# Second layer's keys with values and both query kinds from products of 256 columns, recurrent queries with keys in one; part of VectorE's work on ScalarE

## Time and profile before

| | |
|---|---|
| median of 3 runs | 369.15 us (365.88 to 369.27) |
| profiled execution | 368.68 us, span of its instructions 367.0 us |
| mean granted TensorE clock | 0.863 |
| TensorE matmul, weight load | 299.7 us (82%), 210.4 us |
| VectorE | 243.5 us (66%) |
| ScalarE | 187.5 us (51%) |
| GpSimd | 147.0 us (40%) |

### The profile page before, as it was taken

How to read it: one execution, slowest core, us unless ns; L and a number is a source line. 1 busy time by engine, 2 the same in 40 slices (tenths; PEclk the granted TensorE clock), 3 DMA queues, 4 the chain that set the end, 5 groups by cost and what they waited for, 6 DMA issues and landing times.

```text
span 367.0 us, 7990 instructions
## 1 busy us (share of the span) xinstructions
PE 299.7 (82%) x2646; PEld 210.4 (57%) x2646; DVE 243.5 (66%) x697; ACT 187.5 (51%) x392; POOL 147.0 (40%) x225
## 2 busy tenths in 40 slices
PE   0556898288899987768989889987688999999993
PEld 0432444145559965555645455454445877999993
DVE  5779757288977777589867879999899013431124
ACT  1447987238656541232153676576116775646450
POOL 4955788951133452393024223244562110100272
PEclk9985999799979996678555998999657999999999
DMA  6997000000000660000000000000012625543122
GB/s 199 334 348 329 0 3 2 0 2 1 2 2 0 232 231 0 0 1 2 0 2 0 3 2 2 2 3 8 30 43 68 203 81 159 158 145 87 34 54 80
DMA packets 21383, 26.14 MB, mean 71 GB/s; under 512 B 1816, under 2 KB 16672, under 8 KB 20832
## 3 DMA queue, kind: packets, MB, share of 16 engines
q1 hardware_dynamic: 20576, 24.07, 20.6%
q0 software_dynamic: 768, 1.57, 1.5%
HBM read 19.15 MB, written 6.49 MB: 70 GB/s over the span
## 4 chain that ended last, share of the span: by engine, by line
PE 34%; DVE 12%; issue 6%; ACT 2%; POOL 2%; DMA 2%; SPq 1%; POOLq 1%; DVEq 0%; ACTq 0%
PE single L1668 4%; PE single L1324 4%; PE single L1331 4%; DVE mx L1117 3%; PE double L1371 2%; POOL tmp L787 2%; PE double L1679 2%; PE double L1531 2%; PE single L1679 2%; PE outs L1420 2%; PE double L1527 2%; PE double L1324 1%; PE double L1331 1%; PE double L1596 1%; PE outs L1428 1%
## 5 line engine op out<-in xcount | busy, mean ns | idle before, releaser
L865 ACT ACTIVATE region_p<-double 128x1024 f32<-128x1024 f32 x64 | 63.6, 1030 | 26.8 <-PE double L1371 11.8
L751 POOL TENSOR_SCALAR_AFFINE_SELECT region_p<-region_p 128x512 f32<-128x512 f32 (+1 forms) x48 | 38.8, 808 | 55.7 <-ACT region_p L865 54.3
L1117 DVE TENSOR_REDUCE mx<-double 128x4 f32<-128x1024 f32 (+1 forms) x24 | 29.4, 1226 | 4.5 <-PE double L1531 3.7
L709 POOL TENSOR_SCALAR rstd<-mv 128x2 f32<-128x2 f32 x24 | 5.8, 240 | 65.5 <-DVE mv L990 64.6
L997 DVE TENSOR_SCALAR xn<-x,mv,rstd 128x128 f32<-128x128 f32 x64 | 24.7, 499 | 6.3 <-POOL rstd L715 4.4
L787 POOL DMA_INDIRECT tmp<-moved,spots x12 | 11.5, 961 | 33.9 <-issue 33.5
L1104 DVE TENSOR_REDUCE mxc<-double 128x16 f32<-128x1024 f32 x16 | 19.6, 1225 | 7.8 <-PE double L1511 7.2
L1331 PE MATMUL single<-wb,xnT 128*128 128x128 f32 (+2 forms) x112 | 22.1, 325 | 3.2 <-ACT xnT L820 2.0
L744 POOL TENSOR_SCALAR kcm<-kcT,cst 128x1024 f16<-128x1024 f16 x8 | 22.9, 2863 | 0.8
L1420 PE MATMUL outs<-region_p,vst 128*32 128x256 f32 x256 | 22.9, 440 | 0.2 <-issue 0.2
L1331 PEld LDWEIGHTS single<-wb,xnT 128*128 128x128 f32 x112 | 17.6, 224 | 8.9 <-issue 7.5
(11 more groups left out here) (342 smaller groups left out, 771.5 us busy)
## 6 DMA issues: line engine op xcount, KB each, us to landing
tmp<-in_experts SPq DMA_DIRECT2D x11, 514.0 KB, 3.5
w<-in_experts SPq DMA_DIRECT2D x4, 1024.0 KB, 6.4
moved<-yb SPq DMA_DIRECT2D x1, 3840.0 KB, 17.6
w<-in_w1a SPq DMA_DIRECT2D x2, 1024.0 KB, 15.3
w<-in_w2a SPq DMA_DIRECT2D x2, 1024.0 KB, 10.3
xl<-moved SPq DMA_DIRECT2D x19, 64.0 KB, 3.1
moved<-yb SPq DMA_DIRECT2D x19, 64.0 KB, 2.2
wb<-in_wb SPq DMA_DIRECT2D x1, 837.0 KB, 8.5
```

The lines of the kernel that those rows point to most:

```text
L751: then(g.affine_select(out=v, in_=v, compare_op=ALU.is_ge, fill=0.0, base=0, pattern=[[0, n], [1, P]], channel_multiplier=-1), "prob_masked")
L865: a.activation(probs[:, slot("prob", key), :], psum(step), ACT.Exp, scale=SCALE).then_inc(psum_done[PSUM.slot(step)], 1)
L1117: gives(step, v.tensor_reduce(dst, psum(step).rearrange("p (r g k) -> p r g k", r=2, k=k), X, ALU.max))
```

## The change

- `k4` and `v4` become one step `k4` with a moving operand of 256 columns; VectorE makes the key stack, then ScalarE copies the values out with two instructions. `q4` and `qc4` become one step `q4`: one product of 256 columns, after which VectorE builds both stacks; `tq` of either kind waits for both stacks.
- The biases of the values of both cross attentions and of layer 1's self attention are no longer added to the values: two new steps `vb.1` and `vb.4` push them through the output weights and add them to the output bias, once. `kcv` is then two copies instead of eight additions.
- Norms 3, 4 and 6 (`SCALED`): the normed tiles are made by ScalarE as `x * rstd + offset`; GpSimd makes `offset = -mean * rstd` with two more instructions.
- `p3a` is one product with a 128x128 weight; ScalarE takes out both halves.
- The output gate is `0.5 * tanh(z / 2) + 0.5`: one ScalarE and one VectorE instruction. `mxe` has two instructions instead of three.
- `LENGTHS` has new numbers and more kinds, and `ORDER_OF_STEPS` is a new list. In it ropea.3 and ropea.1 (square roots) stand behind the first exponentials; kcx.1 stands between sc.0.0.5 and sc.0.2.0 (before: between sc.0.3.0 and sc.0.3.1); the mixture of layer 0 for sequences 1 and 3 (fup.2, fup.3, fdown.2, fdown.3) stands inside the recurrent block of 0 and 2 (before: ahead of it). The last steps are nearly the same.

```diff
+SCALED = (3, 4, 6)
-        parts = [("D", 0.9 if twice else 0.5)] + ([("G", 0.7)] if s in (1, 3, 4) else [])
+        parts = [("A" if s in SCALED else "D", 0.9 if twice else 0.5)] + ([("G", 0.7)] if s in (1, 3, 4) else [])
...
+                    if s in SCALED:
+                        mean = mv[:, h, tiles(b), 0].unsqueeze(1).to_broadcast([P, n, 2])
+                        o = offset[:, h, 0:n, tiles(b)]
+                        then(g.tensor_tensor(o, mean, r[:, 0:n], ALU.mult))
+                        then(g.tensor_scalar(o, o, -1.0, None, ALU.mult), "rstd_ready")
...
+                if kind == "lnb" and step[1] in SCALED:
+                    act.wait_ge(sem("rstd_ready"), count(("lna",), ("lna", s, b)))
+                    for n, dst in enumerate((h, 1 - h) if s in AGAIN else (h,)):
+                        for t in tiles_of(b):
+                            ins = a.activation(xn[:, dst, t, :], x[:, t, :], ACT.Identity,
+                                               bias=offset[:, h, n, t:t + 1], scale=rstd[:, h, n, t:t + 1])
...
+                elif kind == "k4":
+                    after_scalar(act, step)
+                    act.wait_ge(sem("presets4"), 4 * count(("presets4",), ("presets4", b)))
+                    for q in range(2):
+                        a.activation(v4[:, tiles(b), q, :, 16 * q:16 * q + HD],
+                                     two(psum(step))[:, :, P:T].rearrange(
+                                         "p i (q h e) -> p i q h e", q=2, e=HD)[:, :, q], ACT.Copy).then_inc(
...
+                    evac(step, kT3[:, slot("mlstm", b), :], psum(step)[DH:2 * DH, 0:T])
...
-                    then(a.activation(og3[:, w], og3[:, w], ACT.Exp, scale=-1.0), "og_exp")
+                    then(a.activation(og3[:, w], og3[:, w], ACT.Tanh, scale=0.5), "og_tanh")
...
-                            ins = v.tensor_tensor(vc[rows, l // 4, m, :, :, 16 * n:16 * n + HD],
-                                                  sel(psum(step)[rows, m * P:(m + 1) * P]),
-                                                  sel(bv[rows, :]), ALU.add)
+                        ins = v.tensor_copy(
+                            dst.rearrange("p m r j e -> p m (r j) e"),
+                            psum(step)[rows, :].rearrange("p (m q h e) -> p m q h e", m=NB, q=2, e=HD)[:, :, n])
...
+                elif kind == "vb":
+                    added = bias({1: "bo1", 4: "bp4"}[b])
+                    ins = v.tensor_tensor(added, added, psum(step)[:, 0:P], ALU.add)
...
-                    then(v.tensor_scalar(m, m, -1.0 / MAXDIV, None, ALU.mult))
-                    then(v.tensor_copy(q[:, :, 24], m))
-                    then(v.tensor_tensor(q[:, :, 25], m, q[:, :, 24], ALU.subtract), "max_ready")
+                    then(v.tensor_scalar(q[:, :, 24], m, -1.0 / MAXDIV, None, ALU.mult))
+                    then(v.scalar_tensor_tensor(q[:, :, 25], m, -1.0 / MAXDIV, q[:, :, 24], ALU.mult,
+                                                ALU.subtract), "max_ready")
...
-                    then(v.tensor_scalar(o, o, 1.0, None, ALU.add))
-                    then(v.reciprocal(o, o), wait=False)
+                    then(v.tensor_scalar(o, o, 0.5, 0.5, ALU.mult, ALU.add), wait=False)
...
-                    for n, w in enumerate(("wq3", "wk3")):
-                        ins = mm(dst[0:DH, n * T:(n + 1) * T], W(w), xnT[:, 1, toks(b)],
-                                 start=True, stop=True)
+                    mm(dst[:, 0:T], W("wqk3"), xnT[:, 1, toks(b)], start=True, stop=True)\
+                        .then_inc(psum_full, 1)
...
-                    w = {"q1": "wq1", "q4": "wq4", "k4": "wk4", "qc4": "wcq4", "v4": "wv4"}[kind]
+                    w = {"q1": "wq1", "q4": "wqq4", "k4": "wkv4"}[kind]
```

More of the change, by code:

```diff
@@ L211, in the_steps @@
         add(("tr3", b), [n], ("P", 0.4), ("A", 0.4))
-        add(("p3a", b), [("tr3", b)] + [("ropeb", n) for n in every], ("P", 1.4), ("A", 0.4), ("D", 1.1))
+        add(("p3a", b), [("tr3", b)] + [("ropeb", n) for n in every], ("P", 1.4), ("A", 0.76))
         add(("p3b", b), [("tr3", b)], ("P", 0.5), ("A", 0.3), ("D", 0.4), ("A", 0.3),
@@ L337, in pair_of @@
 def pair_of(step):
-    if step[0] in ("kck", "kcv", "kct", "kcx", "casts", "presets0", "presets1", "tab"):
+    if step[0] in ("kck", "kcv", "kct", "kcx", "vb", "casts", "presets0", "presets1", "tab"):
         return 0
@@ new lines @@
+fup.1 pv.1.1.1 oc.1.1 tqm.1.3 fdown.0 fdown.1 nxa.0 nxa.2 nxb.0 sc.1.3.0 sc.1.3.1 lna.3.0 ot.1.1
+lnb.3.0 ou.1.1 nxb.2 lna.3.2 pv.1.3.0 kck.4 pv.1.3.1 op.1.1 lna.2.1 oc.1.3 tr3.0 ot.1.3 p3a.0
+presets4.0 p3b.0 ou.1.3 kcv.4 lnb.3.2 rows.0 lnb.2.1 ml.0.0 op.1.3 lna.2.3 tr3.2 ml.0.1 tr2.1 p3a.2
+lnb.2.3 ml.0.2 p3b.2 ml.0.3 lna.4.0 tr2.3 lnb.4.0 xa.1 rows.2 kct.4 xa.3 ml.2.0 tr.4.0 fup.2 k4.0
+ml.2.1 fup.3 ml.2.2 tk4.0 kcx.4 fdown.2 ml.2.3 lna.4.2 q4.0 fdown.3 tq.4.0 nxa.1 lnb.4.2 nxa.3 nxb.1
+lna.3.1 nxb.3 mxs.0.0 tq.5.0 tr.4.2 lnb.3.1 presets4.1 mxs.0.1 k4.2 mxs.0.2 mxs.0.3 tr3.1 tk4.2
@@ L617, in decoder, with normed, stacks @@
         two = lambda ap: ap.rearrange("p (i n) -> p i n", i=2)
-        STACKS = ("ropeb", "kck", "q1", "q4", "k4", "qc4")
+        def normed(eng, step):
+            same = [s for s in ORDER[:INDEX[step] + 1]
+                    if s[0] == "lnb" and (s[1] in SCALED) == (step[1] in SCALED)]
+            eng.wait_ge(sem("xn_scaled" if step[1] in SCALED else "xn_ready"), len(same))
+        def stacks(step):
+            made = {"ropeb": 1, "kck": 1, "q1": 1, "q4": 2, "k4": 1}
+            return sum(made.get(s[0], 0) for s in ORDER[:INDEX[step] + 1])
         block = ctx.enter_context(nc.Block())
@@ L990, in _ @@
                     then(v.bn_aggr(mv[:, h, t1, :], stat[:, h, t1, :]), "var_ready")
-                elif kind == "lnb":
+                elif kind == "lnb" and step[1] not in SCALED:
                     s = step[1]
@@ L1336, in stacked @@
                 pe.wait_ge(sem("ident16_ready"), 1)
-                pe.wait_ge(sem("stack_ready"), count(STACKS, made))
+                pe.wait_ge(sem("stack_ready"), stacks(made))
                 take(step)
@@ L1445, in _ @@
                     pe.wait_ge(sem("ident16_ready"), 1)
-                    pe.wait_ge(sem("stack_ready"), count(STACKS, ("ropeb", b)))
+                    pe.wait_ge(sem("stack_ready"), stacks(("ropeb", b)))
                     pe.wait_ge(sem("k0_ready"), count(("ropeb",), ("ropeb", b)))
```

233 lines of the change are left out of this document (119 added, 114 removed), and 37 rows, old and new, of the table LENGTHS.

## The result

The changed kernel is slower: 374.65 us (median of four runs) against 368.32 us of the kernel before on the same chip, ratio 1.013, 95% interval 1.008 to 1.018; on a second chip 374.97 against 369.20 us, again 1.013 (1.008 to 1.019). The prediction was 360 us with a range of 347 to 373. The profiled execution took 374.53 us (span 372.7), 5.85 us more than the profiled one of before.

The account below looks back on a forecast made before the run. From 100 to 279 us no engine was full: TensorE bounded first, VectorE from 200 us; after 279 us TensorE. Balance -10.8, clock -3, tables +2.6 and norms +2.5 gave -8.7 us on 368.68: 360 us, range 347 to 373.

Parts of the forecast that it names:

- the expert stage, costed at nothing: From 279 us on, TensorE busy 60.64 of 62 us: untouched by the change, moves only as a whole, no cost.
- a longer expert stage, whose order also changed: Sign that the prediction is wrong: the expert stage, expected again at 62 us, comes out longer.
- the four rivals: Clock returns, 350 us (0.14); nothing gained, 367.7 (0.18); ScalarE's queue, ten norms 376 (0.15); tanh tables, 370 (0.02).
- Balance and clock, -10.8 and -3: From 100 to 279 us: TensorE's busy share up to 88%, -10.8 us; fewer holes keep the clock up, -3 us.
- VectorE's relief: 20.5 us of VectorE work taken off, some 18.8 between 100 and 279 us, where VectorE stops being the bound.
- The longer norm, +2.5: Twelve norms each 0.84 us later; three without cover, in the recurrent block and sequence 3, +2.5 us.
- rival 3: ScalarE's queue stands between norm and transposition, 1.87 us per norm; six equal now, ten give 376 us; chance 0.15.
- Table loads, +2.6: Four more table changes on ScalarE, 1.28 us each; only the first two counted, +2.6 us.
- rival 4: tanh lies in another table than exp: two loads for each of four gates, 10.3 us, 370 us; chance 0.02.
- The early stretch, 0: Before 100 us: kcx.1 only changes place, 6 us of hole as now; 0, ends -5 and +5.

Follow-up runs that it names:

- e1: Changed kernel with the steps from xl.0 on in the order of the kernel before (the old tail): 366.97 us, ratio 0.993 to the kernel before.
- e4: Changed kernel with each overflow block's rows loaded ahead of its weights and of the wait for the weight slot: 363.90 us, ratio 0.985.
- e10: Old operations of the kernel before in the new order of the change: 395.22 us, ratio 1.063 to the kernel before.
- e12: The same kernel as e6, run again: 363.17 us, ratio 0.982 to the kernel before.
- e17: The kernel of e12 unaltered, run as a control: 364.26 us, ratio 0.979 to the kernel before.
- e3: Changed kernel in its own order with norms 3, 4 and 6 on VectorE again: 385.76 us, ratio 1.041 to the kernel before.
- e2: All new operations in the old order of the kernel before: 388.11 us, ratio 1.053 to the kernel before.
- e11: e6 with qkv.3, qkv.1, ropea.3 and ropea.1 ahead of the first exponential, two table loads less: 372.97 us, ratio 1.002 to the kernel before.
- e15: e14 with rows loaded first as in e4: 369.38 us, ratio 0.994 to the kernel before.
- e5: The changed kernel once more, unaltered, on a second chip: 374.97 us, ratio 1.013 to the kernel before.
- e6: Changed kernel with both the old tail of e1 and the early rows of e4: 365.06 us, ratio 0.978 to the kernel before.
- e9: Changed kernel in its own order with four weight slots instead of three: 373.77 us, ratio 1.010 to the kernel before.
- e13: Changed kernel, three weight slots, loads from dl.11 on moved ahead of stores on SyncE's queue: 376.27 us, ratio 1.015 to the kernel before.
- e14: e9's four weight slots with loads moved further ahead on SyncE's queue: 371.93 us, ratio 0.987 to the kernel before.

## Why the prediction was wrong

**The step that failed is the expert stage, costed at nothing**: that from 279 us on "nothing that the change touches lies there" and that it "moves only as a whole". I looked at the operations and not at the list. I had also called the last steps nearly the same: that holds for the last 33 or so, but of the 127 ahead of them, back to xl.0, only three stand in their old place counted from the end. The new tail costs 7.8 us in the profile, 6.3 of them idle time of TensorE, which waits 7.9 us for late loads. Every kernel that has it unmended has this stretch (75.5 to 76.6 us in five profiles), and e1, e4 and e10 show it to be the order's. The last paragraph named "a longer expert stage, whose order also changed" as what would be wrong, but gave it neither price nor chance. None of the four rivals is this one. With the stage at 68.8 us the profiled execution would have been at 366.7 us. The sum gave 360.0 for it and 374.5 came: 7.8 us of the 14.5 are this step, 7.0 are the next.

**Balance and clock, -10.8 and -3.** At the first `xl` load the sum promised -8.7 us in all; measured were -1.8. In the profiles in which the full clock is back at 139 us (e1, e4, e12, e17: first load at 268.9 to 269.9) it is -6.7 to -7.7. So the sum up to there was off by 1 to 2 us for the one course of the clock and by 7 for the other, which the changed kernel takes by its times in seven of eight runs; the late return of the clock is some 5 of these 7 us. That the sum is nearly right for the first course is luck in part, since its terms were not measured singly. Of the clock I had foreseen only the gain: 0.61 rose to 0.83 from 140 to 200 us as hoped, but 0.93 fell to 0.76 from 100 to 140 us, where TensorE has 5.9 idle us instead of 2.2. Why TensorE is busy 300 and not 294 us, with 34 instructions less, is not shown: over the whole span the granted clock even rose, from 0.863 to 0.881. The same instructions kept it busy 291.4 us in e4 and 289.4 in e12.

**VectorE's relief.** Right in its total (21.3 us for 20.5), and e3 and e10 confirm that it reaches the time, nearly one to one, in the new order. In the old order it does not (e2).

**The longer norm, +2.5, and rival 3.** The operation is close to what I had: a pair runs 0.87 us in the timeline, not 0.84. Its sum was not: ScalarE's normed tiles take 13.6 us, not 9, because norm 3 has four tiles for each sequence and I had counted a pair. How much of the longer norm lies on the chain was not measured. Then ScalarE's group, and GpSimd's two new ones:

```profile
232.63 0.87 ACT L859 ACTIVATE xn<-x,offset,rstd 128x128 f32<-128x128 f32 x2
```

```profile
L859 ACT ACTIVATE xn<-x,offset,rstd 128x128 f32<-128x128 f32 x32 | 13.6, 483 | 8.1 <-POOL offset L735 7.9
```

```profile
L735 POOL TENSOR_SCALAR offset<-offset 128x2 f32<-128x2 f32 (+1 forms) x12 | 2.9, 245 | 1.1
L734 POOL TENSOR_TENSOR offset<-mv,rstd 128x2 f32<-128x2 f32 (+1 forms) x12 | 2.4, 200 | 0.9
```

But rival 3 fell: with the norms on VectorE the kernel is 10.8 us slower. By the Trainium skill's ratio (Trainium Architecture — The Big Picture, the table of engines: VectorE up to about three times ScalarE's rate) a pair would have taken 1.8 us, an estimate; the rows say 0.87 against 0.60.

**Table loads, +2.6.** Nine, as counted (eight below, one at 0.8 us). Their time is real, but pricing them by themselves was the mistake: the two early ones buy a first exponential 5 us sooner, and e11 shows that trade to be worth some 7 to 10 us.

```profile
L906 ACT ACT_TABLE_LOAD x4 | 5.1, 1283 | 0.1
L879 ACT ACT_TABLE_LOAD x2 | 2.6, 1283 | 2.7 <-DVE tmp L1051 2.7
L927 ACT ACT_TABLE_LOAD x2 | 2.6, 1283 | 1.7 <-issue 1.7
```

No load stands at the gate's four tanh, and rival 4 is out. For the three behind exponentials that is what the Trainium skill says (ScalarE: Activation LUTs, Table sets: tanh lies in the set of exp). The fourth, at 180.48 us, stands behind a GELU and takes no load either.

**The early stretch, 0.** About right in size, but not in its reason. kcx.1 holds GpSimd from 34.49 to 46.28 us, and TensorE waits 5.4 us there in four pieces, where it was one wait of 6.27. The first three, 4.8 us, are by the trace for ScalarE, whose two added table loads of this stretch stand at 36.60 and 40.90 us; only the last, of 0.62 us, is for GpSimd's masks:

```profile
40.98 0.75 PE L1395 MATMUL double<-qkT 32*128 32x512 f16 x4 [2.37 <-ACT qkT L843]
43.36 0.61 PE L1395 MATMUL double<-qkT 32*128 32x512 f16 x2 [1.63 <-ACT region_p L906]
44.76 0.61 PE L1395 MATMUL double<-qkT 32*128 32x512 f16 x2 [0.80 <-ACT region_p L906]
```

## What to carry to other kernels

A change that comes with a new order of steps has changed every stage, also those whose instructions stayed: compare the two lists there too, above all how much work lies between what frees a buffer and what needs its next load, and price it. Operations and their order are one thing: here each fit its partner, and crossing them cost 20 us either way. Where a small load opens a chain (transposition, copy, product) and a large one is needed only at its end, issue the small one first; this one edit turned the change from 1.3% slower to 1.5% faster, and with the old tail to 1.8%. Of the 11 us between the first two medians the stage accounts for 7.0; most of the rest I put down to the clock, which in e4's profile comes back early (first scatter 4.9 us sooner).

## What the runs showed of the hardware

- TensorE's instructions from 130.6 to 138.7 us start within 0.01 us of each other in the changed kernel and in e4, and are followed by 12 us more at half clock in the one and by full clock at once in the other. Five executions profiled had full clock from 139 us on (e1, e4, e12, e15, e17), six were at half until 149 or 151 us (changed, e5, e6, e9, e13, e14). It was worth 4.9 us of 370, 1.3%. The Trainium skill (TensorE: Matmul & The Clock Gate, Part 1) speaks of the ramp at a kernel's start, calls it run-variable and puts it at less than 1% of a typical span; here a return of the clock in the middle of the kernel makes more.
- 64 KB land 3.2 us after issue behind 514 KB on the same queue (changed kernel) and 1.8 us ahead of them (e4), medians of eleven loads each.
- An ACTIVATE of 128x128 with scale and bias per partition takes 480 ns at the median (477 to 494), where one of 128x128 from PSUM with a bias takes 380 in the mean.
- An ACTIVATE with tanh starts without a table load behind exponentials (126.80, 139.35 and 203.79 us) and behind GELU (180.48 us); the exponential after the latter takes one (181.92 us).
